# Graph-attention kernel on one core: mean of the values summed by TensorE, four tokens to a partition, bias rows earlier, last stores on ScalarE's queue

## What is computed

```
hs, ht = layer_norm(x), layer_norm(h_target)          # ln1 scale and bias
q, k, v = ht @ Wq + bq, hs @ Wk + bk, hs @ Wv + bv
logits = q . k per head / sqrt(32), -1e30 where adj[t, s] == 0
ctx = softmax(logits) @ v
ht = layer_norm(ht + ctx @ Wo + bo)                   # ln2 scale and bias
out = normalise(x + nodemask * (ht + gelu(ht @ W1) @ W2))
```

## Time and profile before

| | us |
|---|---|
| median of 3 runs | 292.06 (291.75 to 292.36) |
| the profiled execution, its own time | 291.37 |
| its span, first to last instruction | 289.6 |
| busy: PE / DVE / POOL / ACT | 223.8 / 212.3 / 185.2 / 172.5 |
| mean granted TensorE clock | 0.921 of full |

### The profile page before, as it was taken

One profiled execution on the slowest core, in us unless ns is written; L12 is line 12 of the kernel. 1 busy time (PEld: TensorE's weight loads), 2 busy tenths in 40 slices (PEclk: granted clock), 3 DMA queues, 4 the chain that ended last, 5 costly groups with the idle time before them and its releaser, 6 DMA issues.

```text
span 289.6 us, 4175 instructions
## 1 busy us (share of the span) xinstructions
PE 223.8 (77%) x1316; PEld 176.1 (61%) x1319; DVE 212.3 (73%) x614; ACT 172.5 (60%) x322; POOL 185.2 (64%) x205
## 2 busy tenths in 40 slices
PE   7397988841304876998889889997699899597990
PEld 7243443310202564997879768986589798496980
DVE  2444999999824875795977869899979988798111
ACT  2589999920504476776866798686376534353420
POOL 8581526981068768788887867888757687046542
PEclk9899999985555799999999999999979999999996
DMA  5999999999985536656555645556662455112120
GB/s 167 357 400 414 416 414 412 407 353 343 391 281 169 140 104 191 190 155 169 157 155 170 177 131 154 144 158 177 178 180 74 111 147 148 33 38 72 36 72 27
DMA packets 23457, 58.03 MB, mean 200 GB/s; under 512 B 4019, under 2 KB 12485, under 8 KB 21382
## 3 DMA queue, kind: packets, MB, share of 16 engines
q0 software_dynamic: 8368, 27.01, 32.5%
q1 hardware_dynamic: 14228, 29.91, 27.4%
q10 hardware_dynamic: 834, 0.79, 1.0%
HBM read 51.40 MB, written 10.49 MB: 214 GB/s over the span
## 4 chain that ended last, share of the span: by engine, by line
DVE 31%; POOL 25%; PE 16%; issue 9%; ACT 9%; DMA 8%; SPq 1%; POOLq 0%; ACTq 0%; DVEq 0%
POOL arena L775 16%; PE bank L1032 6%; ACT arena L1228 4%; PE score L1023 4%; DVE arena L1730 4%; POOL tab L765 4%; POOL rstd_late L795 4%; DMA tab<-in_x_dram 3%; DVE arena L1736 3%; DMA arena<-kv_scratch,places 3%; DVE cand L1520 2%; ACT tab L1211 2%; DVE logits L1691 2%; DVE arena L1689 2%; DMA tab<-tab_scratch,places 2%
## 5 line engine op out<-in xcount | busy, mean ns | idle before, releaser
L775 POOL DMA_INDIRECT arena<-kv_scratch,places x79 | 87.6, 1109 | 22.2 <-issue 22.2
L1023 PE MATMUL score<-h_t,w_sb 128*128 128x128 f32 x512 | 62.3, 275 | 0.0
L1032 PE MATMUL bank<-w_sb,gelu_t 128*128 128x256 f32 x256 | 61.8, 386 | 0.0
L1023 PEld LDWEIGHTS score<-h_t,w_sb 128*128 128x128 f32 x512 | 60.0, 192 | 0.6 <-ACT h_t L1363 0.3
L1032 PEld LDWEIGHTS bank<-w_sb,gelu_t 128*128 128x128 f32 x256 | 48.1, 195 | 5.9
L1309 ACT ACTIVATE gelu_t<-score 128x512 f32<-128x512 f32 x32 | 19.1, 597 | 26.6 <-PE score L1023 26.4
L795 POOL TENSOR_TENSOR rstd_late<-var_late,minus_half 128x1 f32<-128x1 f32 (+3 forms) x23 | 21.2, 922 | 20.9 <-DVE var_late L1799 20.6
L883 PE MATMUL bank<-tab,arena 128*128 128x512 f32 x64 | 30.2, 617 | 3.1 <-ACT arena L1219 1.8
L765 POOL DMA_INDIRECT tab<-tab_scratch,places x16 | 17.9, 1119 | 19.3 <-DVE place_value L1658 15.0
L1689 DVE TENSOR_TENSOR arena<-arena,query 128x1024 f32<-128x1024 f32 (+3 forms) x22 | 24.5, 1112 | 4.4 <-DMA arena<-kv_scratch,places 2.5
L1691 DVE TENSOR_REDUCE logits<-arena 128x32 f32<-128x1024 f32 (+3 forms) x22 | 24.4, 1110 | 0.8
(11 more groups left out here) (153 smaller groups left out, 425.7 us busy)
## 6 DMA issues: line engine op xcount, KB each, us to landing
arena<-in_adj_dram SPq DMA_DIRECT2D x6, 1024.0 KB, 12.0
w_sb<-in_adj_dram SPq DMA_DIRECT2D x6, 1024.0 KB, 13.1
kv_scratch<-arena SPq DMA_DIRECT2D x8, 512.0 KB, 10.4
tab<-in_x_dram SPq DMA_DIRECT2D x4, 512.0 KB, 11.3
own_t<-in_adj_dram SPq DMA_DIRECT2D x2, 1024.0 KB, 11.7
gelu_t<-in_adj_dram SPq DMA_DIRECT2D x2, 1024.0 KB, 10.9
tab_scratch<-in_L_gnn_h_target_dram SPq DMA_DIRECT2D x1, 2048.0 KB, 16.9
tab_scratch<-in_x_dram SPq DMA_DIRECT2D x1, 2048.0 KB, 20.7
```

What stands on the lines that cost most here:

```text
L775: pool.indirect_dma_start(kv_ring[:, ring_at[m] + j, :], None, kv_dram[:, :], at).then_inc(gathered[m][piece], 16)
L1023: mm = pe.matmul(hid_ps[(2 * n + half) % 3][:, f % 4 * P:(f % 4 + 1) * P], w1_sb[:, k, f * P:(f + 1) * P], h2_t[:, n % 2, k, :], start=(k ...
L1032: pe.matmul(ff_ps[:, 0:D], gelu_t[:, n % 2, f, :], w2_sb[:, f, :], start=(f == 0), stop=False, skip_group_check=True)
```

## The change

Five edits:

1. **Tokens four to a partition.** Partition p of chunk c holds tokens 512c + 4p to 512c + 4p + 3. A chunk's load and two tiles' `save_kv` now move 4 KB runs instead of 1 KB and 2 KB ones. The node mask must lie the same way: it is loaded once, as 512 runs of 16 bytes, where the row-wise load of 16 runs of 512 bytes stood, and the second mask load and PE's turning of the mask (line 915) are gone.
2. **Mean by TensorE.** `add_v` and `v_total` are gone; PE sums the 16 value tiles by 16 matrix products into one bank behind the last `make_keys`.
3. **POOL's order.** With `add_v` gone the constants follow the fourth `rsqrt1` with no wait, and the bias rows stand behind the first quarter's split, not the second's.
4. **Last stores on ACT's queue.** The last three `save_kv` are issued by ACT: two behind the last `find_edges`, one behind the edge counts.
5. **Wq.** Its load stands ahead of all stores on SP's queue (before, behind them); DVE scales it ahead of the wait for `placed` (before, after the places were written).

```
-                sp.dma_start(tok[:, c, :, :], x.rearrange("(c t p) d -> p c t d", p=P, t=CT)[:, c, :, :]).then_inc(x_loaded[c], 16)
+                sp.dma_start(tok[:, c, :, :], x.rearrange("(c p t) d -> p c t d", p=P, t=CT)[:, c, :, :]).then_inc(x_loaded[c], 16)
-            sp.dma_start(node_i[:, :], nodemask.rearrange("(t p) -> t p", p=P)).then_inc(node_loaded, 16)
+            sp.dma_start(node_target[:, :, :], nodemask.rearrange("(q u b) -> u q b", q=QUARTERS, b=UB),
+                         allow_slow_non_contiguous=True).then_inc(node_loaded, 16)
...
-            sp.dma_start(node_target[:, :, :], nodemask.rearrange("(q u b) -> u q b", q=QUARTERS, b=UB),
-                         allow_slow_non_contiguous=True).then_inc(target_loaded, 16)
             for t in range(12, TILES):
                 load_adj(t)
+            sp.dma_start(wq_sb[:, :, :], Wq.rearrange("(k p) n -> p k n", p=P)).then_inc(wq_loaded, 16)
             for t in range(0, TILES - 6, 2):
-                save_kv(t)
+                save_kv(sp, t)
...
-            for t in range(TILES - 6, TILES, 2):
-                save_kv(t)
-            sp.dma_start(wq_sb[:, :, :], Wq.rearrange("(k p) n -> p k n", p=P)).then_inc(wq_loaded, 16)
...
+        def save_kv(eng, t):
+            eng.wait_ge(kv_read, t + 2)
+            c, i = t // CT, t % CT
+            rows = kv_dram[1 + c * CH:1 + (c + 1) * CH, :].rearrange("(p i) n -> p i n", i=CT)
+            eng.dma_start(rows[:, i:i + 2, :], kv_out[:, t:t + 2, :]).then_inc(kv_saved, 16)
...
             def project_mean():
                 pe.wait_ge(const_ready, 6)
-                pe.wait_ge(v_added, TILES)
-                pe.wait_ge(keys_read, QK * QUARTERS)
-                pe.matmul(mean_ps[0:CW, 0:D], mean_ones[:, :], v_total[:, :], start=True, stop=True).then_inc(mean_projected, 1)
+                pe.wait_ge(h_copied, 2 * DK * CHUNKS)
+                for t in range(TILES):
+                    pe.wait_ge(kv_read, t + 1)
+                    mm = pe.matmul(mean_ps[0:CW, 0:D], mean_ones[:, :], kv_out[:, t, D:KV], start=(t == 0), stop=(t == TILES - 1))
+                mm.then_inc(mean_projected, 1)
...
             find_edges(15)
+            save_kv(act, TILES - 6)
+            save_kv(act, TILES - 4)
             for q in range(QUARTERS - 1):
                 act.wait_ge(pick_step, PER_LIST * (q + 1))
...
+            save_kv(act, TILES - 2)
             act.wait_ge(const_ready, 6)
             act.wait_ge(mean_projected, 1)
...
+            dve.wait_ge(wq_loaded, 16)
+            dve.tensor_scalar(wq_sb[:, :, :], wq_sb[:, :, :], Q_SCALE, None, ALU.mult).then_inc(node_ready, 1)
             dve.wait_ge(placed, 1)
```

More of the change, by code:

```diff
@@ L137, in graph_attention @@
         target_number = sb("target_number", [P, CELLS], I32)
-        node_i = sb("node_i", [TILES, P], I32)
-        node_rows = sb("node_rows", [TILES, P])
+        node_natural = sb("node_natural", [P, TILES])
         node = sb("node", [P, TILES])
@@ L285, in graph_attention @@
         ctxt_ps, attn_ps, h2t_ps, ff_ps, hid_ps, own_ps = banks[0], banks[1], banks[2], banks[3], banks[4:7], banks[7]
-        class_ps, rank_ps, place_ps, mean_ps, tally_ps = banks[4], banks[5], banks[6], banks[7], banks[4]
+        class_ps, rank_ps, place_ps, mean_ps, tally_ps = banks[4], banks[5], banks[6], banks[0], banks[4]
         turned = bank[0:2]
@@ L304, in graph_attention @@
         const_ready = sem("const_ready")
-        node_turned = sem("node_turned")
+        natural_loaded = sem("natural_loaded")
+        natural_ready = sem("natural_ready")
         node_ready = sem("node_ready")
@@ L609, in _ @@
                 sp.wait_ge(late_done, ENGINES)
+                sp.dma_start(node_target[:, :, :].rearrange("p q b -> p (q b)"), nodemask.rearrange("(t p) -> p t", p=P),
+                             allow_slow_non_contiguous=True).then_inc(natural_loaded, 16)
                 kv_all = kv_dram[1:N + 1, :].rearrange("(t p) n -> p t n", p=P)
@@ L667, in rsqrt1 @@
                 pool.tensor_tensor(shift[:, c, :], minus_mean[:, c, :], rstd[:, c, :], ALU.mult).then_inc(rstd_ready, 1)
[L669 to L681, removed]
             def wait_listing(q):
@@ L731, in _ @@
             pool.tensor_copy(ext[:, :, 0], target_number[:, :]).then_inc(target_ready, 1)
-            pool.wait_ge(target_loaded, 16)
-            pool.tensor_scalar(ext[:, :, 1], node_target[:, :, :].rearrange("p q b -> p (q b)"), 1.0, None,
-                               ALU.is_equal).then_inc(target_ready, 1)
-            add_v(1)
-            wait_listing(1)
+            pool.wait_ge(node_ready, 1)
+            pool.tensor_copy(ext[:, :, 1], node[:, :]).then_inc(target_ready, 1)
             pool.memset(bias_rows[:, :], 0.0).then_inc(bias_step, 1)
             pool.wait_ge(bias_loaded, 32)
+            wait_listing(0)
             pool.tensor_scalar(bqo[:, 0:D], bqo[:, 0:D], Q_SCALE, None, ALU.mult).then_inc(bias_step, 1)
@@ L749, in _ @@
             pool.sem_inc(bias_ready, 1)
-            add_v(2)
-            add_v(3)
             def fetch(m, j):
@@ L924, in _ @@
             turn_rows(2)
-            pe.wait_ge(node_ready, 2)
             make_keys(0)
@@ L942, in _ @@
             classes_flat = in_class[:, :, :].rearrange("p k c -> p (k c)")
+            pe.wait_ge(keys_read, QK * QUARTERS)
             pe.wait_ge(classed, 1)
@@ L981, in project_query @@
                     pe.wait_ge(bias_ready, 2)
-                    pe.wait_ge(node_ready, 3)
+                    pe.wait_ge(node_ready, 2)
                 pe.wait_ge(own_copied, DK * (o + 1))
@@ L1554, in _ @@
             dve.wait_ge(node_loaded, 16)
-            dve.tensor_scalar(node_rows[:, :], node_i[:, :], 1.0, None, ALU.is_equal).then_inc(node_ready, 1)
+            dve.tensor_scalar(node[:, :], node_target[:, :, :].rearrange("p q b -> p (q b)"), 1.0, None,
+                              ALU.is_equal).then_inc(node_ready, 1)
             unit_stats(1)
-            dve.wait_ge(node_turned, 1)
-            dve.tensor_copy(node[:, :], banks[7][:, 0:TILES]).then_inc(node_ready, 1)
-            dve.wait_ge(node_ready, 2)
+            dve.wait_ge(node_ready, 1)
             dve.wait_ge(bkv_loaded, 32)
@@ L1947, in attend @@
                             normalise(GROUPS * t - 1, 1, None)
+                dve.wait_ge(natural_loaded, 16)
+                dve.tensor_scalar(node_natural[:, :], node_target[:, :, :].rearrange("p q b -> p (q b)"), 1.0, None,
+                                  ALU.is_equal).then_inc(natural_ready, 1)
+                dve.wait_ge(natural_ready, 1)
                 for o in range(TILES, 2 * TILES):
```

16 lines of the change are left out of this document (1 added, 15 removed).

## The result

The changed kernel takes **296.45 us** (median of 4 runs, 295.72 to 297.17) against 292.21 us of the kernel before, measured beside it (4 runs, 291.75 to 293.10). The ratio is 1.0122 with an interval of 1.0062 to 1.0183: slower by some 1.2%. The forecast was 289.4, its range ended at 292.1. The profiled execution took 297.17 us, its span is 295.3; the mean granted TensorE clock fell from 0.921 to 0.908.

What follows compares the result with a forecast made beforehand. The prediction took the chain of waits up to the first gather at 81.11 us as the bound, with DVE held up by POOL. Terms -1.57 - 1.61 + 0.35 + 0.2 = -2.63 gave 289.4 us from 292.06; range 287.8 to 292.1.

Steps and rivals of the forecast that it cites:

- Splits (-1.57, -1.61): DVE's splits of quarters 1 and 2 fall to 1.79 us each without POOL's work beside them: -1.57 and -1.61 us.
- Rival D: DVE's splits: the contention isn't POOL's, long instructions stay, 292.3 us; chance 0.04.
- Bias rows (+0.35): POOL's bias rows, now earlier, end at 46.1 us and their last copy overlaps quarter 1's split: up to +0.35 us.
- Chunk and mask loads (+0.2): Start of the kernel: 512 small mask runs ahead of the second chunk's load delay ACT's second normalise by 0.2 us.
- Mean on PE (0): Sixteen products on PE, 3.5 or 6.9 us, end before 70 us in PE's idle time before the ranking: cost 0.
- Wq and the issues on ACT (0 and 0): DVE's 0.43 us scaling of Wq fits before a wait for PE; ACT's three store issues hold nothing up: 0 each.
- rival A: SP's queue: the mask load blocks the second chunk, landing after 15.2 us, up to +4.5 us, 293.4; chance 0.14.
- The pile of transfers: DMA before the first gather: copy of x becomes last, landing at 78.45 us with Wq's +0.75; no cost of its own.
- the other bound: Before the first gather: the time POOL itself is ready, forecast at 78.5 us.
- C: More than the sum: early start, shorter pile of transfers, TensorE's clock rising earlier; gain 3.8 us, 288.3; chance 0.13.
- Rival B: First gather: Wq and the earlier stores push the copies' end to 80 us; gain 1.1, 291.0 us; chance 0.12.

Runs made afterwards that it cites:

- mean_only: The kernel before with only the mean moved to PE (POOL's sums gone), layout, bias rows, stores and Wq as before; 292.60 us, ratio 0.9965.
- stores_sp: The changed kernel with the last three stores back on SP's queue behind the two copies; 291.23 us, ratio 0.9905.
- after_again: The changed kernel run and profiled once more, unaltered, on another chip; 294.46 us, ratio 1.0044 to the kernel before.
- weights_wait: mask_late with SP's queue waiting for the first gather to land before it loads Wo, W1 and W2; 294.74 us, ratio 1.0068.
- before_again: The kernel before, unaltered, profiled a second time on a chip where everything takes 5 us longer; 298.30 us, ratio 1.0008.
- copies_first: The changed kernel with the two table copies issued ahead of SP's five stores, ACT's stores left alone; 291.79 us, ratio 0.9948.
- mask_late: stores_sp with the mask's load behind the second chunk's and DVE's mask compare behind that chunk's statistics; 290.01 us, ratio 0.9889.

## Why the prediction was wrong

**Splits (-1.57, -1.61).** Right. Measured 2.16 us for the forecast 3.36 - 1.57 + 0.35 = 2.14, and 1.67 for 1.79; mean_only isolates the sums' part. Rival D falls.

**Bias rows (+0.35).** Right. The last bias copy runs from 46.35 to 46.95 and the cast beside it takes 0.59 for 0.22: +0.37. The Trainium skill (SBUF — State Buffer, Who interferes with whom) calls the shared ports an exclusive lock; the trace agrees, since a step that works on one partition held a cast of 128 (0.59 us for 0.22).

**Chunk and mask loads (+0.2).** Wrong in sign for the loads: DVE's statistics of the second chunk began at 11.40 for 11.98, far from rival A's 15.2, and ACT's second normalise came 0.6 us earlier (14.96 for 15.56). The gain was lost again: the quarter-1 split began 0.69 us late, at 46.45, since PE's first 16 rows of projections ran longer at half clock, a term that the forecast did not have. In stores_sp, with the same loads, the split began at 45.47; in mean_only, with the loads of before, the 16 rows took 9.28 us (8.05 before), so the loads do not set this. The sixteen rows of the two kernels, changed kernel first, then stores_sp:

```profile
13.43 10.07 PE bank L860 x16
```

```profile
13.89 8.62 PE L862 MATMUL bank<-tab,arena 128*128 128x512 f32 x16 [0.32 <-ACT arena L1198]
```

**Mean on PE (0).** Right in cost, wrong in size: the trace has 32 rows for the 16 products (a row counts each float32 product twice), 7.07 us at full clock, and not 3.5. The cover held, 2.89 us of it left:

```profile
60.89 7.07 PE L885 MATMUL bank<-arena,mean_ones 128*32 128x256 f32 x32
70.85 0.16 PE L921 MATMUL score<-ones_bf,in_class 128*128 128x1 bf16 x1 [2.89 <-DVE in_class L1592]
```

**Wq and the issues on ACT (0 and 0).** Right: the scaling (0.40) is followed by a wait of 0.56 for PE, the issues took 0.33 each at 55.17, 56.46 and 62.03, amid ACT's other work.

Taken together, POOL would have been ready 0.57 us behind the places, at 78.34. The forecast said 78.5. That it fits is partly luck: the places came 2.18 us earlier, not 2.63, and the rest is that the first gather follows the places by 0.57 us where it was 1.16 before (79.95 to 81.11). mean_only has 0.57 as well, so this comes with the sums' removal; the forecast did not have it.

**The pile of transfers: the failed step.** The forecast said that moving stores to another queue "changes their order, not the end of the pile: the copy becomes the last", landing at 78.45, and so "costs nothing of its own". Three things were wrong in it:

- The landing is no single number. It was 80.63 and 78.46 in two profiles. I computed one value, found it 0.05 us ahead of the other bound, and gave that meeting no width. The second profile met the value, the first missed it by 2.2 us: 0.89 because the copy was issued later (50.95 for 50.06), 1.3 because it took longer.
- Release is not start. The gather starts 0.89 us behind the copy's landing (80.63 to 81.52, 78.46 to 79.35). So even the forecast landing would have given 79.3.
- The gather itself got slower by 1.3 us (5.74 and 5.77 for 4.49), since it now starts while transfers still fill the engines (a share of 1.01 and 1.10 in 81 to 85 us, 0.92 and 0.84 before). The prediction moved the gather without asking what it lands beside. Even with the gather early, in stores_sp, it takes 5.89, and 3.82 us of head start (81.11 to 77.29) become 2.34 at the statistics.

For after_again the sum is then: gather -1.76, statistics -0.41, first `h` +0.34. The 2.2 us that DVE won are gone before the first `h`. In the profile of the result, statistics +1.73 and first `h` +3.62, most of the 4.2 us between the medians (the two profiled executions differ by 5.8). Of this, 1.9 us arise between the statistics and `h`, where the trace shows the clock as the difference: at half since 70.6, it was full again only at 104.7 us; in the profile before, from 97.3. It rose at 99.5 in after_again and at 95.4 in stores_sp.

**Rival A** fell with the second chunk, and of C only the early chunk came. **Rival B** named the mechanism, the copies' end near 80 us, and had it at 0.12. Its argument against was "the pile is the same bytes but for wq". The bytes were indeed the same; their order decided, and who waits for which. Its price of 291.0 lacked the slower gather and the 0.89.

**The late stage.** None of its instructions changed, and the prediction let it move along unchanged. Its length, from the first `h` to the end of the span, was 187.4 before and 189.5 in the changed kernel, but 186.7 to 190.8 across the others on the first chips, weights_wait aside, and 192.7 to 197.1 on the third chip, with before_again at 195.0. The stretches at half clock differ in number and place: two profiles of the changed kernel had three such stretches behind 110 us, mean_only and the first profile of before one, stores_sp two, before_again three (a fall in the last 5 us of the span is not counted). That the change makes them more likely is not shown. The granted clock of the timed executions speaks weakly against it, as it is a mean over the whole span: 0.919 over 12 executions of the changed kernel (after_again), 0.910 over 34 of the kernel before beside them. On the first two chips the timed medians follow the first `h` to within about 1.3 us all the same: -2.35 against -1.9 in stores_sp, -2.25 against -1.1 in copies_first, +2.63 against +1.9 in weights_wait.

**A version that beats both** is the change with the copy kept ahead: stores_sp or, by the best ratio, mask_late at 0.9889 (0.9853 to 0.9925), 290.0 us beside 292.9.

## What to carry to other kernels

When stores move to a second queue, ask which transfer the next stage waits for, and where that one stands: where both had work in 60 to 63 us they got equal numbers of packets, so the one with the larger packets took most of the engines, and whatever is last on the first queue pays. The same bytes in another order are a different kernel; issue the transfer that gates the next stage first, since it may need nothing but its source. And where a forecast lets two bounds meet within a few tenths, write down their spread, and price what the released instruction will land beside.

## What the runs showed of the hardware

- Two queues with work moved packets one for one (183 and 179 in 60 to 63 us), although the one had little more than 1 MB queued and the other some 4 MB. With packets of 3.7 KB against 1.3 KB the shares of the engines were 81.0% and 28.8%. SP's queue moved 0.24 MB there, and 0.88 with the engines to itself.
- A first gather that starts beside other transfers takes longer: 3.7 us at a DMA share of 0.13 to 0.43 (weights_wait), 4.5 at 0.92 and 0.84 (before), 5.8 at 1.04 to 1.06 (mask_late).
- The copies' small packets are slow and not of one price. With full engines, 4 KB packets went at 417 GB/s (57 to 60 us, changed kernel). In 69 to 72 us the changed kernel moved only 217 GB/s at a DMA share of 1.11, stores_sp 377 at 1.07. What makes the same kind of packet slower in the one is open.
- One step of POOL on one partition delays a DVE cast of 128 partitions for most of the time that it still runs (46.95 - 46.45 = 0.50 us left, cast 0.37 longer).
- The number and place of TensorE's half-clock stretches differ between profiles of one kernel (one late stretch, then three, for the kernel before), and eight equal rows then take 1.73 us or up to 3.40:

```profile
118.46 3.40 PE bank L1009 x8
```
